# Moving the softmax division of a causal attention from the probabilities to z, one transposed reciprocal tile per 512 queries and head pair

## The reference

```python
xn = layernorm(x)
K, Q, V = (einsum('bpd,ihd->biph', xn, W) for W in (W_K, W_Q, W_V))   # 16 heads, 64 wide
scores = where(tril, einsum('biph,biqh->biqp', K, Q), -1e10)
attn = softmax(scores / 8, axis=-1)
z = einsum('biph,biqp->biqh', V, attn)
out = einsum('bqf,df->bqd', z_flat, W_O)
# mixture of 9 experts, the 2 best for each token, weights renormalised:
ffn = sum over experts of cw * ((silu(xn Wg) * (xn Wu)) Wd)
return x + out + ffn
```

## Time and profile before

| | us |
|---|---|
| median of 3 runs | 811.46 (810.71 to 814.54) |
| the profiled execution | 817.95 |
| its span, first to last instruction | 816.1 |
| PE busy / DVE busy / ACT busy / POOL busy | 700.7 / 634.5 / 560.7 / 502.5 |

### The profile page before, as it was taken

How to read it: one execution, slowest core, us unless ns; L and a number is a source line. 1 busy time by engine, 2 the same in 40 slices (tenths; PEclk the granted TensorE clock), 3 DMA queues, 4 the chain that set the end, 5 groups by cost and what they waited for, 6 DMA issues and landing times.

```text
span 816.1 us, 15653 instructions
## 1 busy us (share of the span) xinstructions
PE 700.7 (86%) x4241; PEld 565.4 (69%) x4241; DVE 634.5 (78%) x1374; ACT 560.7 (69%) x1311; POOL 502.5 (62%) x517
## 2 busy tenths in 40 slices
PE   5406999988889898989898989898989999988875
PEld 4306999867667676777777777776767777766663
DVE  5934777677868887888787978888888888887772
ACT  4414555567767777787777777787877787876771
POOL 5294444079896565656565656565656666678892
PEclk9856999999999999999999999999999999999996
DMA  6138222235252525242524334251607061525011
GB/s 195 55 105 179 75 61 59 41 78 122 62 127 47 113 55 114 51 106 51 112 63 94 79 85 99 58 120 44 141 16 159 16 142 33 124 62 117 27 26 30
DMA packets 35478, 68.27 MB, mean 84 GB/s; under 512 B 5264, under 2 KB 26096, under 8 KB 31344
## 3 DMA queue, kind: packets, MB, share of 16 engines
q1 hardware_dynamic: 33136, 63.08, 34.0%
q0 software_dynamic: 2304, 4.72, 2.5%
HBM read 12.73 MB, written 4.72 MB: 21 GB/s over the span
## 4 chain that ended last, share of the span: by engine, by line
POOL 38%; issue 26%; PE 19%; DVE 7%; DMA 4%; ACT 3%; SPq 1%; POOLq 1%; DVEq 0%; ACTq 0%
POOL probs L562 26%; POOL k_parts L498 4%; POOL z_lo L567 4%; DMA k_st<-k_parts 4%; PE ps_big L1114 2%; PE ps_z L1135 2%; PE ps_z L1136 2%; PE ps_big L1168 2%; PE ps_big L1115 2%; PE ps_big L1116 2%; PE ps_mid L1125 2%; PE ps_z L1198 1%; PE ps_z L1197 1%; PE ps_mid L1181 1%; ACT probs L704 1%
## 5 line engine op out<-in xcount | busy, mean ns | idle before, releaser
L562 POOL TENSOR_TENSOR probs<-probs,rden 128x128 f32<-128x128 f32 (+7 forms) x256 | 293.9, 1148 | 189.8 <-DVE rden L950 188.1
L963 DVE TENSOR_TENSOR pT_lo<-ps_mid,pT_hi 128x512 fp32r<-128x512 f32 (+3 forms) x384 | 200.9, 550 | 40.8 <-ACT pT_hi L719 39.0
L719 ACT ACTIVATE pT_hi<-ps_mid 128x512 fp32r<-128x512 f32 (+3 forms) x384 | 174.5, 491 | 70.4 <-PE ps_mid L1181 68.5
L1168 PE MATMUL ps_big<-k_st,q_st 128*128 128x512 f32 (+2 forms) x768 | 218.9, 386 | 0.0
L1181 PE MATMUL ps_mid<-ident,probs 128*128 128x128 f32 x1152 | 176.7, 279 | 37.0 <-DVE pT_lo L963 25.4
L704 ACT ACTIVATE probs<-ps_big,neg_max 128x128 f32<-128x128 f32 (+7 forms) x256 | 190.2, 743 | 15.4 <-DVE neg_max L945 14.2
L945 DVE TENSOR_REDUCE neg_max<-ps_big 128x1 f32<-128x128 f32 (+7 forms) x256 | 191.1, 747 | 1.8 <-PE ps_big L1168 1.1
L1181 PEld LDWEIGHTS ps_mid<-ident,probs 128*128 128x128 f32 x1152 | 133.6, 141 | 80.6 <-DVE pT_lo L963 40.1
L1197 PE MATMUL ps_z<-pT_hi,v_st 128*128 128x512 f32 (+2 forms) x384 | 133.3, 354 | 0.0
L1198 PE MATMUL ps_z<-pT_lo,v_st 128*128 128x512 f32 (+2 forms) x384 | 130.1, 353 | 0.0
L1168 PEld LDWEIGHTS ps_big<-k_st,q_st 128*128 128x128 f32 x768 | 118.4, 194 | 1.4 <-ACT probs L704 0.2
(11 more groups left out here) (190 smaller groups left out, 1093.8 us busy)
## 6 DMA issues: line engine op xcount, KB each, us to landing
k_st<-k_parts SPq DMA_DIRECT2D x64, 512.0 KB, 8.4
q_st<-q_parts SPq DMA_DIRECT2D x64, 256.0 KB, 4.5
y_dram<-y_sb SPq DMA_DIRECT2D x40, 64.0 KB, 1.5
raw_gu<-in_L_ffn_Wg_dram SPq DMA_DIRECT2D x9, 176.0 KB, 2.4
raw_gu<-in_L_ffn_Wu_dram SPq DMA_DIRECT2D x9, 176.0 KB, 2.5
raw_d<-in_L_ffn_Wd_dram SPq DMA_DIRECT2D x9, 128.0 KB, 2.6
res<-in_L_attn_x_dram SPq DMA_DIRECT2D x4, 256.0 KB, 3.6
xn_dram<-xn SPq DMA_DIRECT2D x4, 256.0 KB, 2.9
```

The costliest lines, as they stand in the source:

```text
L562: pool.tensor_tensor(rows, rows, col.to_broadcast([P, width]), ALU.mult).then_inc(normed, 1)
L719: nc.scalar.activation(pT_hi[j][buf][:, g * TPB:g * TPB + tiles, (i % TPB) * P:(i % TPB + 1) * P], ps_mid[:, bank, 0:tiles * P].rearrange( ...
L963: nc.vector.tensor_tensor(pT_lo[j][buf][:, kt, q], ps_mid[:, bank, 0:tiles * P].rearrange("p (t q) -> p t q", t=tiles), pT_hi[j][buf][:, k ...
L1168: ins = nc.tensor.matmul(ps_big[:, n % 2, c0:c1], w, k_st[half][h][:, part, c0 - off:c1 - off], start=part == 0 and not masked, stop=part ...
```

## The change

The probabilities are left as they come from the exponential, so the turned blocks, their residues and the products with V are those of unnormalised rows. `recip` now runs twice in a half (slots 12 and 15), on the 8 sums (4 query tiles, 2 heads) of one block of 512 queries. POOL spreads the 8 columns to a 128x512 tile (`spread_rden`), PE transposes that in four 128x128 blocks into `ps_misc` (`turn_rden`, slots 13 and 18), and DVE multiplies z by it before z is split (`scale_z`, others of the same slots). `norm` is gone. Because `turn_rden` needs `ps_misc` in slot 18, which is slot 2 of the next half, q0, q1, k0, k1 and v0 move to later slots. `y_sb` shares its memory with `rden_wide`.

```diff
-        PROJ_SLOT = {"wqkv": 1, "q0": 2, "q1": 3, "k0": 4, "k1": 6, "v0": 7, "v1": 9, "t0": 11, "t1": 12, "wo": 14}
+        PROJ_SLOT = {"wqkv": 1, "q0": 3, "q1": 4, "k0": 6, "k1": 7, "v0": 8, "v1": 9, "t0": 11, "t1": 12, "wo": 14}
+        SCALE_SLOT = [UPH - 3, UPH + 2]
+        RECIP_SLOT = [UPH - 4, UPH - 1]
+                    events.append((SCALE_SLOT[j], ("scale", (b, j))))
...
-            def norm(p, n):
...
-                pool.wait_ge(rden_done, unit_count(p, n))
-                pool.tensor_tensor(rows, rows, col.to_broadcast([P, width]), ALU.mult).then_inc(normed, 1)
+            def spread_rden(p, b, j):
+
+                pool.wait_ge(rden_done, o_count(p, b, j))
+                wait(pool, rden_turned, o_count(p, b, j) - 1)
+                cols = den_of(rden, b)[:, :, TPB * j:TPB * (j + 1)].rearrange("p h u -> p u h")
+                pool.tensor_tensor(rden_wide[:].rearrange("p u (h c) -> p u h c", h=2), cols.unsqueeze(3).to_broadcast([P, TPB, 2, DH]),
+                                   one_col[:].unsqueeze(1).unsqueeze(1).to_broadcast([P, TPB, 2, DH]), ALU.mult).then_inc(rden_spread, 1)
...
-                act.wait_ge(z_summed, z_count(p, b, 1, j))
+                act.wait_ge(z_scaled, o_count(p, b, j))
...
-            def recip(p, n):
-                dve.wait_ge(exp_done, unit_count(p, n))
-                nc.vector.reciprocal(rden[:, n:n + 1], den[:, n:n + 1]).then_inc(rden_done, 1)
+            def recip(p, b, j):
+
+                dve.wait_ge(exp_done, unit_count(p, b * UPH + QT + TPB * (j + 1) - 1))
+                cols = slice(TPB * j, TPB * (j + 1))
+                nc.vector.reciprocal(den_of(rden, b)[:, :, cols], den_of(den, b)[:, :, cols]).then_inc(rden_done, 1)
+
+            def scale_z(p, b, j):
+
+                dve.wait_ge(rden_turned, o_count(p, b, j))
+                dve.wait_ge(z_summed, z_count(p, b, 1, j))
+                nc.vector.tensor_tensor(z_sum[j][:], ps_misc[:, :], z_sum[j][:], ALU.mult).then_inc(z_scaled, 1)
...
             def turn_probs(p, n):
                 i = ORDER[n % QT]
-                pe.wait_ge(normed, unit_count(p, n))
+                pe.wait_ge(exp_done, unit_count(p, n))
...
+            def turn_rden(p, b, j):
+
+                misc_free()
+                pe.wait_ge(rden_spread, o_count(p, b, j))
+                for u in range(TPB):
+                    c = ORDER[TPB * j + u] % TPB
+                    ins = nc.tensor.transpose(ps_misc[:, c * P:(c + 1) * P], rden_wide[:, u, :], ident[:])
+                ins.then_inc(rden_turned, 1)
+                last_misc.append((z_scaled, o_count(p, b, j)))
```

More of the change, by code:

```diff
@@ L95, in bass_layernorm_causal_attention_plus_moe_kernel @@
         eps_col = sb("eps_col", [P, 1])
+        one_col = sb("one_col", [P, 1])
         unused = sb("unused", [P, 3])
@@ L98, in bass_layernorm_causal_attention_plus_moe_kernel @@
         raw_o = sb("raw_o", [P, P])
-        y_sb = [sb(f"y_sb{j}", [P, D]) for j in range(4)]
+        early = ExitStack()
+        y_sb = [sb(f"y_sb{j}", [P, D], stack=early) for j in range(4)]
+        early.close()
+        rden_wide = sb("rden_wide", [P, TPB, 2 * DH])
         yg = [sb(f"yg{j}", [P, D]) for j in range(4)]
@@ L224, in bass_layernorm_causal_attention_plus_moe_kernel @@
         s_ready = sem("s_ready"); max_done = sem("max_done"); exp_done = sem("exp_done")
-        rden_done = sem("rden_done"); normed = sem("normed")
+        rden_done = sem("rden_done"); rden_spread = sem("rden_spread"); rden_turned = sem("rden_turned"); z_scaled = sem("z_scaled")
         t_ready = sem("t_ready"); pT_copied = sem("pT_copied"); pT_split = sem("pT_split")
@@ L349, in last_unit, with den_of @@
             return max(u for u in range(QT) if ORDER[u] // TPB == j)
+        def den_of(t, b):
+            return t[:, b * UPH:(b + 1) * UPH].rearrange("p (h u) -> p h u", h=2)
         def score_cols(i):
@@ L463, in _ @@
                                pattern=[[-1, E], [1, E]], channel_multiplier=0).then_inc(const_made, 1)
+            pool.memset(one_col[:], 1.0)
             pool.memset(ones_bf[:], 1.0).then_inc(const_made, 1)
@@ L554, in gather_y @@
                     add_y(c, TT - 1)
-            def norm(p, n):
-                width = (ORDER[n % QT] + 1) * P
-                rows = probs[n % 4][:, 0:width]
-                col = rden[:, n:n + 1]
-                pool.wait_ge(rden_done, unit_count(p, n))
-                pool.tensor_tensor(rows, rows, col.to_broadcast([P, width]), ALU.mult).then_inc(normed, 1)
+            def spread_rden(p, b, j):
[4 more added lines that the diff above has]
+                                   one_col[:].unsqueeze(1).unsqueeze(1).to_broadcast([P, TPB, 2, DH]), ALU.mult).then_inc(rden_spread, 1)
             def split_z(p, b, j):
@@ L575, in split_others @@
                         split_z(p if b >= 0 else p - 1, b % 2, j)
-            norm(0, 0)
             def iteration(p, first, last):
@@ L581, in iteration @@
                 for s in range(2 * UPH):
[L582 to L586, removed]
+                    b, turn = divmod(s, UPH)
+                    if turn in RECIP_SLOT:
+                        spread_rden(p, b, RECIP_SLOT.index(turn))
                     split_others(p, plan[s - 1])
@@ L993, in split_others @@
                         sum_z(p if b >= 0 else p - 1, b % 2, h, j)
+                    if kind == "scale":
+                        b, j = arg
+                        scale_z(p if b >= 0 else p - 1, b % 2, j)
                     if kind == "proj":
@@ L1006, in iteration @@
                 for s in range(2 * UPH):
-                    n = s + AHEAD - 2
-                    if n < 2 * UPH:
-                        recip(p, n)
-                    elif not last:
-                        recip(p + 1, n - 2 * UPH)
+                    b, turn = divmod(s, UPH)
+                    if turn in RECIP_SLOT:
+                        recip(p, b, RECIP_SLOT.index(turn))
                     n = s + AHEAD - 1
@@ L1250, in others @@
                         project(p, arg, 1 - arg // 9)
+                    if kind == "scale":
+                        b, j = arg
+                        turn_rden(p if b >= 0 else p - 1, b % 2, j)
                     if kind == "o":
```

1 line of the change is left out of this document (removed).

## The result

The changed kernel takes 866.9 us (median of four runs, 865.3 to 867.6) where the kernel before takes 811.7 beside it: 1.065 times as long, with a 95% interval of 1.060 to 1.070. The forecast was 847, at most 862. So the direction was right, and the size was missed by 20 us, outside the range.

What follows compares the result with a forecast made beforehand. Each half was taken to stand on the landing of the k stack's DMA. Twelve halves at +2.2 us gave +26, clock drops +13, ends -3: +36 on a median of 811.46, so 847 us, range 822 to 862.

Steps and rivals of the forecast that it cites:

- The moved slot and the k stack: k1 from slot 6 to 7: k stack issued later, PE waits 1.5 to 2 us in slot 13; +2.2 a half.
- Together 0: Parts added or removed from slot 13 to k1 in slot 7 cancel: 0 a half, ends -0.7 and +0.7.
- The cast's lock: DVE's roundings shorten without `norm` on POOL; counted in full, a half 0.6 us shorter than forecast, time 840.
- the term of 0.6 us off DVE in slot 5: q1's split (0.68) replaces k0's rounding (1.31) in slot 5: 0.6 off DVE, nearly all beside PE's own work.
- The clock: Slot 13 waits: a drop costs 1.44 us, three drops in four waits; +1.1 a half, +13 us.
- the second rival: Every wait for the k stack loses the clock: +40, 851 us; chance 0.2.
- The ends: Outside the loop: last half shorter without `norm`, other k stacks 0, last `scale_z` +0.7, first unit -0.7; -3 us.
- Faster: Stretch from slot 13 to slot 7 shrinks by more than the slot's 2.2 us: 796 us; chance 0.1.
- The rival that put `scale_z` behind late transposes: POOL's spread late, `scale_z` waits, up to 1 us in both places: +24, 870; worse than forecast's range, chance 0.05.
- the last line of the sum: +36 on the profiled 817.95 gives 854; the median is 6.5 lower, the same 36 on 811.46 gives 847.

Runs made afterwards that it cites:

- b_slots: The kernel before with only the new, later projection slots (q0 3, q1 4, k0 6, k1 7, v0 8): 851.8 us.
- n_slots_head: a_head with the division left out altogether (no spread, turns, multiplication or reciprocals), new slots kept: 797.3 us.
- a_head: The changed kernel with the wait for the k stack split by heads, each head's scores waiting for its own DMAs: 829.7 us.
- r_head: b_head without `norm` on POOL, the 256 reciprocals kept, so the division is left out of the result: 793.6 us.
- b_head: The kernel before with the wait for the k stack split by heads, each head's scores waiting for its own DMAs: 807.4 us.
- b_slots_head: b_slots with the wait for the k stack split by heads: 822.1 us.
- n_head: n_slots_head with the projection slots of the kernel before, division still left out: 783.5 us.
- s_head: a_head with only the multiplication on DVE kept (z times one), spread and turns left out: 830.2 us.
- s_late: s_head with the multiplication moved behind the split of the turned probabilities on DVE: 833.0 us.

## Why the prediction was right in its direction and wrong in its size

**The sum that the runs give.** From the medians, one change of a chain at a time: two-part wait -4, new slots +15, `norm` and reciprocals out -25, scaling in +32, k stack's joint wait back +37; together +55. The prediction had the same parts in another grouping, so I go by its steps.

**The moved slot and the k stack: right.** The 12 us from issue to matmul stayed 12.13; k1's place to the issue took 3.36 (predicted 3.5); PE waited 1.52 to 1.81 us in slot 13 of eleven of the loop's twelve halves (predicted 1.5 to 2), and 3.07 in the first. b_slots, with this step alone, has halves of 41.2 to 41.4 us at full clock, where 38.87 + 2.2 is 41.07.

**"Together 0": wrong, and the step that failed.** The stretch from slot 13 to the issue grew by 3.46, not 2.2: 2.54 for the moved slot less 0.51 for the chain behind k1 (0.16 less than forecast), and 1.4 to 1.5 for the rest, where I had 0. Together the stretch is 1.3 us a half over the forecast, some 16 us in twelve halves. Counted from the slot 13 matmul of each kernel (588.12 and 477.57), the changed kernel is later
- by 0.44 from where `turn_rden` stands among PE's matmuls in slot 13; I had it covered by ACT's move and DVE's sum of z, 0 of a bound of 0 to 0.4;
- by 0.67 at the turns of slot 15 (592.74 against 481.52), 0.23 more at the residues behind `scale_z`;
- by 1.01 in the output product of slot 0 (596.12 against 484.56), where POOL's spread stands ahead of `z_lo`. I had called the spread hidden because its reader comes late. It was hidden from its reader, but not from what was queued behind it on POOL;
- by 1.08 at the projection of slot 3 (604.27 against 492.64): 0.26 had come back in slot 2, and PE's q0 waits 0.34 us for the second multiplication;
- by 1.56 at the output product in slot 5 (609.14 against 497.03, from 0.99 just ahead of it), which waits for q1's split on DVE. I had booked that split as a gain of DVE and not asked who waits for the bank that it frees;
- by 1.48 at k1 (614.96 against 502.93).

The experiments give the sizes with no k stack in the way: multiplication +1.5 a half at full clock (2.03 with the drops), turns and spread +0.25 beside it (+0.75 alone), reciprocals -0.65, `norm` -0.17, new slots +1.22. My terms were +0.6 to 0.7 for the multiplication, 0 for turns and spread, up to -0.9 for the reciprocals, -0.1 for `norm`, and for the slots +2.2 through the k stack only. The reciprocals and `norm` in the loop were about right; the multiplication was sized at less than half of what it cost. It comes twice a half, and the second one, in slot 3, I had priced at 0 to 0.1.

**The cast's lock.** DVE's rounding of k took 422 ns in the mean in the changed kernel where it took 950 before (32 each):

```profile
L795 DVE CAST k_parts<-part_raw 128x512 fp32r<-128x512 f32 x32 | 13.4, 422 | 0.9
```

So the term of 0.6 us off DVE in slot 5 was real: the Trainium skill, "SBUF — State Buffer", section "Who interferes with whom", agrees with this trace. The time that counting it in full would give, 840, did not come; no run shows how much of DVE's gain there reached PE.

**The clock: right in price, wrong in number.** In the changed kernel a drop costs 1.0 to 1.5 us (halves of 43.40 to 43.85 against 42.4), near the 1.44 forecast. But four of the eleven waits of 1.52 to 1.81 us had one, where I took three in four. The loop's first wait, 3.07 us, lost the clock as well, for 7 us (granted 0.54 from 243.0 to 250.0), and its half takes 45.43; so did the waits of 3.01 and 2.85 us outside the loop (198.23 and 802.11). Two stretches of the changed kernel right behind slot 13 (columns as in the earlier trace rows):

```profile
588.00:592.00 4.00, 3.47 (x26) 3.17 (x26) 1.77 (x5) 1.80 (x5) 0.00 (x0) 1.00 0.01 2
...
502.50:505.50 3.00, 3.00 (x13) 2.81 (x13) 0.29 (x1) 0.24 (x1) 0.00 (x0) 0.51 0.00 0
```

The first, behind a wait of 1.74 us, kept 1.00 (2.4 GHz); the second fell to 0.51 (1.2 GHz). So the four drops brought 5 us and the first half 3, of which 1.2 are its later k stack, together 8 where I had 13. The error has the other sign than the first, and hid a part of it. Of the second rival, and of the Trainium skill's "HAM oscillation — how this bites in real kernels" ("TensorE: Matmul & The Clock Gate") behind it, a loss in each turn, this trace shows five in twelve.

**The ends: wrong.** I had -3; the start and the rest came out 3.5 us longer than before. The largest term is the scaling, which I had at +0.7: from n_slots_head to a_head the start grows by 1.7 and the rest by 9.3 (224.23 to 225.94 and 105.2 to 114.5). `norm`'s removal was worth more there than I took: 4 us in the start and 5 in the rest (r_head against b_head). The new slots cost 4 us in the start (b_slots_head against b_head). In the first pair too the k stack is waited for: with the two-part wait after's start falls from 230.05 to 225.94 and its rest from 119.0 to 114.5.

**Adding up.** Loop: 12 x 3.5 = 42 at full clock, where I had 26, and 8 for the clock and the first half, where I had 13; together the 50 measured over steady halves of 38.87 (12 x (43.06 - 38.87)), against 39. Ends: +3.5, where I had -3. The slow start of the profiled execution of before takes 4 of these 53.5 back, which leaves the 49.7 measured against 36. That is 14 of the 20 us missed. The other 6 are in the last line of the sum: the median of before lies 6.5 below its profiled execution, that of after only 0.7 below its own, so that carrying a difference of two profiled executions over to a median was itself worth 6 us. The slow start may be four of them; no other execution of before was profiled.

**The rivals.** "Faster" needed the stretch to shrink; with the old slots, the two-part wait and no division at all it did (37.92, n_head). The rival that put `scale_z` behind late transposes (870) gives nearly the measured time but not the mechanism: POOL's spread was done long ahead of its transposes.

**What stays open.** Why four of eleven waits of 1.52 to 1.81 us lost the clock and the others did not: 1.67, 1.71, 1.72 and 1.81 did, 1.74 twice did not. What the multiplication costs in a place that delays neither `pT_lo` nor ACT's copies. And whether a cheaper place for the scaling, another engine than DVE with the turned sums kept outside the shared bank, would beat 807 us: it wasn't tried, and n_head's 783.5 only shows the room below.

## What to carry to other kernels

Moving work to once per 512 queries makes it smaller in total, but what counts is the place where it lands: here 294 us of POOL's time that mostly hid beside TensorE, and 41 us of reciprocals, were exchanged for 22 us of multiplications on DVE, in slots where TensorE was already waiting for DVE, and 33 us of spreads on POOL. Before moving a producer by one slot, read how long its transfer takes and when its first part is needed; if the parts of a transfer have readers at different times, give each its own semaphore. For each instruction put into an in-order queue, ask not only whether its reader gets it in time, but who reads what is queued behind it, and who waits for the bank that it holds.

## What the runs showed that I had not expected

- Costs in one stretch aren't additive: turns and spread 0.75 us a half alone, 0.25 at full clock beside a multiplication that makes TensorE wait anyway.
- One DVE instruction of 0.69 us costs about the same on either side of its neighbour (40.5 and 40.65 us a half at full clock), but through different queues: once DVE's, once ACT's. The same move costs 26 us in all where the instruction also holds a PSUM bank, most of it in halves that lost the clock.
- Equal means can hide unequal things: of s_head's twelve halves (40.88 us) five lost the clock and took 41.4 to 41.5, of s_late's (40.87) two, which took 41.9 and 43.3.
- The same edit of a wait is worth 37 us where the transfer had become late by 1.5 to 2 us a half, and 5 us where it was just in time.
- A wait of 1.74 us can leave the granted clock at 1.00 (588.12), though one of 0.96 us lost it in the kernel before.
